# A graph layer on one Trainium2 core: edges of one destination packed three to a lane in place of two

## The chip, the cores and the metric

The kernel runs on one core of one Trainium2 chip. The metric is the time of one execution on the device in microseconds (us). TensorE is called PE below, VectorE DVE, ScalarE ACT, GpSimd POOL and SyncE SP. An engine name with a q behind it (SPq) is that engine's own instruction queue.

## The reference

There are 1250 nodes with rows of 1024 floats, 20000 edges `src -> dst`, and a type from 0 to 7 for each edge. Two layers follow each other, each with a residual and a layer norm.

```python
# layer 0: relational graph layer with a gate
out = x @ root + bias
for r in range(8):
    mask = (edge_type == r)
    sums = segment_sum(x[src] * mask[:, None], dst, num_segments=n)
    cnt = segment_sum(mask, dst, num_segments=n)
    out = out + (sums / maximum(cnt, 1.0)[:, None]) @ weight[r]
u = out
z = concatenate([u, x], axis=1) @ w_gate + b_gate
h = tanh(u) * z + x * (1.0 - z)
x = layernorm(x + h)
# layer 1: GCN, with a self loop at every node
dinv = rsqrt(deg)
msg = (x @ W)[src] * (dinv[src] * dinv[dst])[:, None]
x = layernorm(x + relu(segment_sum(msg, dst, num_segments=n) + b))
```

## The kernel before

**Products.** The kernel first forms `y = x @ weight[r]` for all eight types, a half of 512 columns at a time, and writes it to memory as rows. Then an edge's message is one row of `y`, picked by its type and source, times the share 1/cnt that belongs to its destination and type. Every product in 32-bit floats is done as three matmuls of a high and a low part (`xhi`, `xlo`, `whi`, `wlo`). A tile of 128 nodes by 512 columns is therefore 24 matmuls on PE (L790), and PE's program is written as a list of **steps**, each of them a half tile of 12 such matmuls (`half_tile`). Everything else that PE does is placed at the end of a step by tables from step to work (`spread`). DVE and ACT walk the same steps in programs of their own and come `LEAD` = 2 steps earlier with messages. ACT copies a finished tile out of PSUM (`evac`, L1095) and makes `whi` of the next weights (L1088), DVE makes `wlo` (L1310).

**Sorting the edges.** Early on, DVE and PE sort the edges by destination. All edges of one destination are put on lanes (partitions) of a group of 128 destinations. Two edges of one destination share a lane: 128 lanes by two edges are a **pair**. `NPAIR` = 92 pairs hold all edges whatever the draw, `ETILES` = 2 * 92 = 184 is the number of records per lane, and unused places hold an index out of range (`FAR`), for which a gather moves nothing.

**Counting (steps 150 to 215).** For layer 1 a matrix of counts, source by destination, is summed up. POOL makes a one-hot tile of the sources (`src_hot`, L685), DVE one of the destinations (`count_hot`, L1525), PE multiplies the two (`count_pair`, L802: four matmuls of 320 columns a pair), ACT takes the result as integers (`take_counts`, L1132), and DVE adds them to `COUNT` (`count_add`, L1535).

**Messages (run 0 at steps 229 to 314 for the left half of the columns, run 1 at steps 324 to 412 for the right half).** For each pair POOL issues two indirect DMAs (L711) that gather 128 rows of `y` each into one of eight row buffers `raw`. ACT scales the first row by its edge's share (`scale_row`, L1113). DVE multiplies the second by its share and adds the first (`msg_sum`, L1542). Then it makes the one-hot tile of the destinations, `ONEHOT` (L1544). ACT makes the high part of the sum (`msg_high`, L1119), DVE the low part (`msg_low`, L1549). PE multiplies both by the one-hot tile (`message_pair`, L813 and L814: one matmul of 512 columns each), and DVE adds PE's result to the sums `U` three pairs later (`msg_add`, L1556).

**What orders it.** Row buffer r is gathered into again once row r has been used: the first row of a pair when `msg_sum` has read it (`pair_summed`), the second when `msg_low` has (`msg_split`). So POOL is at most eight rows ahead. ACT's `message` scales the first row of the *next* pair before it makes the high part of this one. Ahead of the first pair of run 0, DVE waits for a small transposition (`deg_max_turned`, L925) that PE does at the start of step 229. Run 1 reads rows that exist only when the last tile of the right half, that of step 319, is stored; and its gathers start no earlier than that store. Behind the messages come the gate product (L886), the gate (L952), the product of layer 1 (L979) and its sums (L1045).

Of the kernel before, what the change touches and what calls it, by code (L numbers as in the profile page):

```python
# [28 lines left out]
I16 = mybir.dt.int16  # L29
# [4 lines left out]
P = 128  # L34
# [8 lines left out]
NPAIR = (E // 2 + N // 2 + NT * (P - 1)) // P  # L43
ETILES = 2 * NPAIR
# [10 lines left out]
HIGH_CELL = 1 << 16  # L55
SPLIT = 1024
EXACT = 256
AHEAD = 2
HOTS = 8
EARLY = 5  # L60
SLOTS = 4

# [14 lines left out]
RUN1_FROM, RUN1_TO = 324, 413  # L77
# [6 lines left out]

def spread(start, end, count=NPAIR):
# [6 lines left out]
COUNT_GROUPS = NPAIR // 2  # L92
COUNT_PAIRS = {s: range(2 * these.start, 2 * these.stop) for s, these in spread(COUNT_FROM, COUNT_TO, COUNT_GROUPS).items()}
RUN0_PAIRS = spread(RUN0_FROM, RUN0_TO)
RUN1_PAIRS = spread(RUN1_FROM, RUN1_TO)


def ahead(pairs):

    return {s - LEAD: these for s, these in pairs.items()}  # L100
# [14 lines left out]
def gnn_resnorm_kernel(nc, x, src, dst, edge_type, w_rel, w_root, b_root, w_gate, b_gate, w_gcn, b_gcn, out):  # L115
# [8 lines left out]
    count_d = dram("edge_count", (P, NT * NPAD), I16)  # L124
# [6 lines left out]
    with ctx:  # L131
# [56 lines left out]
        CIN = [place("CIN0", [P, NPAD], I16, "raw_w"), place("CIN1", [P, NPAD], I16, "stage")]  # L188

        U = WORK[:, 0:NT * HW].rearrange("p (g n) -> p g n", g=NT)  # L190
        COUNT = WORK[:, 0:NT * NPAD // 2].bitcast(I16).rearrange("p (g n) -> p g n", g=NT)
# [76 lines left out]
        O_HALF = field("O_HALF", [EPART, CHUNK], I32)  # L268
# [9 lines left out]
        GROUP = small("GROUP", [1, NPAIR], I32)  # L278
        DINV = small("DINV", [P, NT], F32)

        SRC_LOC = place("SRC_LOC", [P, ETILES], F32, "early")
        CELL = place("CELL", [P, ETILES], F32, "early", 4 * ETILES)
        ADDR = place("ADDR", [EPART, ECOL], I32, "early", 8 * ETILES)
        COLS = place("COLS", [P, NCOL], F16, "early", 8 * ETILES + 4 * ECOL)
# [11 lines left out]
        PAIRSUM = place("PAIRSUM", [1, 2, NPAIR], F32, "onehot", 1024)  # L296
# [51 lines left out]
        got = [sem(f"got{b}") for b in range(2 * SLOTS)]  # L348
        row_scaled = sem("row_scaled")
        pair_summed = sem("pair_summed")  # L350
        msg_hi = sem("msg_hi")
        msg_split = sem("msg_split")
        pair_ready = sem("pair_ready")
        pair_done = sem("pair_done")
        pair_added = sem("pair_added")
# [108 lines left out]
        def _(sp):  # L464
# [56 lines left out]
            def load_gate(t):  # L521
                if t == 0:
                    sp.wait_ge(pair_done, 2 * NPAIR)
# [38 lines left out]
            sp.wait_ge(msg_split, 2 * NPAIR - 2)  # L562
            load_root(0)
            sp.wait_ge(msg_split, 2 * NPAIR - 1)
# [727 lines left out]
        def _(dve):  # L1292
# [274 lines left out]
            def count_step(pair):  # L1567
                group, odd = divmod(pair, 2)
                if odd:
                    return  # L1570
# [330 lines left out]
```

## Time and profile before

| | before |
|---|---|
| median of 3 runs | 1624.74 us (1624.61 to 1626.62) |
| the profiled execution | span 1624.1 us from the first to the last instruction; granted PE clock 0.996 of full speed |
| PE busy | 98% of the span |
| DVE, ACT, POOL busy | 69%, 35%, 52% |
| chain that ended last | 93% on PE |

The profile gives the span of its execution; what lies outside it is taken as the 0.6 us between that span and the median. A PE that is shown as busy is not yet a PE that is needed at every instant, because a matmul's time as shown overlaps with that of the next one. Where its matmuls follow each other without an idle gap, the distance between their starts is what one costs.

### The profile page before, as it was taken

What the parts mean: (1) busy time and instruction counts of PE and PEld (TensorE: products, weight loads), DVE (VectorE), ACT (ScalarE), POOL (GpSimd) and SP (SyncE); (2) the same over time, 40 slices, a digit from 0 to 9 for tenths busy, and PEclk for the clock granted to TensorE, in tenths of its full rate; (3) what the DMA queues carried; (4) which work ended last, traced back from release to release, by engine and by line L of the source; (5) the groups of instructions that cost most, each with busy time, mean ns of one, the idle gap of its engine ahead of it and who ended that gap; (6) DMA issues with size and microseconds to landing.
All of it is one profiled execution on the core that took longest, in us unless ns stands there. A gap on an engine that the chain in (4) does not pass through costs nothing.

```text
span 1624.1 us, 23696 instructions
## 1 busy us (share of the span) xinstructions
PE 1597.2 (98%) x7947; PEld 1308.5 (81%) x7947; DVE 1127.3 (69%) x1894; ACT 575.9 (35%) x963; POOL 838.1 (52%) x823
## 2 busy tenths in 40 slices
PE   8999999999999999999999999999999998999997
PEld 7888888888877777788888888888888876888886
DVE  4856655655457667748878785778788869767486
ACT  4211111111133434425655553555555652222000
POOL 1000777777766666537777772777676601222000
PEclk9999999999999999999999999999999999999999
DMA  6322444444322121267777874777778785666643
GB/s 236 103 87 81 129 115 131 112 108 141 83 79 79 59 78 64 67 229 226 247 234 219 250 222 143 236 238 228 231 227 279 273 292 171 238 215 225 267 145 117
DMA packets 122124, 280.34 MB, mean 173 GB/s; under 512 B 23143, under 2 KB 24407, under 8 KB 121873
## 3 DMA queue, kind: packets, MB, share of 16 engines
q0 software_dynamic: 38256, 104.17, 22.3%
q1 hardware_dynamic: 46912, 98.19, 18.8%
q10 hardware_dynamic: 36832, 76.44, 12.5%
q8 instruction: 65, 1.06, 0.3%
q14 instruction: 59, 0.48, 0.1%
HBM read 209.97 MB, written 83.10 MB: 180 GB/s over the span
## 4 chain that ended last, share of the span: by engine, by line
PE 93%; DVE 3%; DMA 2%; issue 1%; ACT 0%; POOL 0%; SPq 0%; ACTq 0%; DVEq 0%; POOLq 0%
PE PG L790 67%; PE PG L979 6%; PE PG L1045 5%; PE PM L802 3%; PE PG L886 3%; PE PM L813 3%; PE PM L814 3%; PE PG L952 2%; DMA y<-STAGE 1%; PE PM L848 1%; PE PM L831 1%; PE PM L772 0%; DMA WRAW<-in_L_gnn_weight_dram 0%; PE PM L961 0%; DMA XROWS<-in_x_dram 0%
## 5 line engine op out<-in xcount | busy, mean ns | idle before, releaser
L790 PE MATMUL PG<-WHI,XHI 128*128 128x512 f32 x1600 | 631.7, 395 | 2.2 <-DVE WLO L1310 2.2
L790 PE MATMUL PG<-WHI,XLO 128*128 128x512 f32 x1600 | 623.5, 390 | 0.0
L790 PE MATMUL PG<-WLO,XHI 128*128 128x512 f32 x1600 | 623.0, 389 | 0.0
L790 PEld LDWEIGHTS PG<-WHI,XHI 128*128 128x128 f32 x1600 | 300.9, 188 | 64.5 <-issue 2.5
L790 PEld LDWEIGHTS PG<-WHI,XLO 128*128 128x128 f32 x1600 | 300.6, 188 | 63.7
L790 PEld LDWEIGHTS PG<-WLO,XHI 128*128 128x128 f32 x1600 | 301.0, 188 | 60.0
L1095 ACT ACTIVATE STAGE<-PG 128x512 f32<-128x512 f32 x200 | 119.1, 596 | 452.8 <-PE PG L790 452.6
L1310 DVE TENSOR_TENSOR WLO<-WRAW,WHI 128x512 fp32r<-128x512 f32 x176 | 122.1, 694 | 223.4 <-ACT WHI L1088 223.1
L711 POOL DMA_INDIRECT WORK<-y,REC x184 | 202.7, 1102 | 91.7 <-issue 49.3
L658 POOL DMA_INDIRECT records<-RREC,IDX x160 | 210.1, 1313 | 61.0 <-issue 43.7
L711 POOL DMA_INDIRECT RAW<-y,REC x184 | 204.2, 1110 | 70.4 <-issue 48.0
L685 POOL TENSOR_SCALAR SRCHOT<-IOTA,SRC_LOC 128x128 bf16<-128x128 f16 x184 | 148.6, 822 | 79.7 <-PE PM L802 79.6
L1556 DVE TENSOR_TENSOR WORK<-WORK,PM 128x512 f32 x184 | 125.3, 681 | 11.5 <-PE PM L814 9.6
L746 POOL TENSOR_TENSOR RSTD<-VAR,MINUS_HALF 128x1 f32<-128x1 f32 x20 | 11.0, 550 | 212.5 <-DVE VAR L1701 212.5
L1535 DVE TENSOR_TENSOR WORK<-WORK,TALLY 128x1280 int16 x92 | 76.7, 833 | 60.5 <-DVE WORK L1535 35.0
L1088 ACT ACTIVATE WHI<-WRAW 128x512 fp32r<-128x512 f32 x176 | 110.1, 626 | 7.7 <-DMA WRAW<-in_L_gnn_weight_dram 3.6
L1132 ACT ACTIVATE TALLY<-PM 128x640 int32<-128x640 f32 x92 | 59.9, 703 | 121.1 <-PE PM L802 121.1
L1119 ACT ACTIVATE SPHI<-WORK 128x512 fp32r<-128x512 f32 x92 | 57.9, 629 | 66.9 <-DVE WORK L1542 66.7
L644 POOL DMA_DIRECT2D EDGE_ROWS<-edge_rows x10 | 7.7, 769 | 141.8 <-DVE ADDR L1459 94.7
L1119 ACT ACTIVATE SPHI<-RAW 128x512 fp32r<-128x512 f32 x92 | 57.9, 630 | 63.9 <-DVE RAW L1542 63.0
L1549 DVE TENSOR_TENSOR SPLO<-WORK,SPHI 128x512 fp32r<-128x512 f32 x92 | 64.3, 699 | 20.0 <-ACT SPHI L1119 17.4
L1113 ACT ACTIVATE RAW<-RAW,REC 128x512 f32<-128x512 f32 x92 | 66.0, 717 | 33.6 <-DMA RAW<-y,REC 29.5
(265 smaller groups left out, 2257.3 us busy)
## 6 DMA issues: line engine op xcount, KB each, us to landing
y<-STAGE ACTq DMA_DIRECT2D x220, 256.0 KB
WRAW<-in_L_gnn_weight_dram SPq DMA_DIRECT2D x128, 256.0 KB, 3.2
EDGE_ROWS<-edge_rows POOLq DMA_DIRECT2D x10, 1000.0 KB, 6.2
WRAW<-in_L_gnn_w_gate_dram SPq DMA_DIRECT2D x32, 256.0 KB, 4.2
WORK<-y SPq DMA_DIRECT2D x15, 512.0 KB, 4.4
WORK<-x SPq DMA_DIRECT2D x10, 512.0 KB, 4.7
WORK<-in_x_dram SPq DMA_DIRECT2D x9, 512.0 KB, 3.7
XROWS<-in_x_dram SPq DMA_DIRECT2D x9, 512.0 KB
```

What stands on the lines that cost most here:

```text
L658: pool.indirect_dma_start(out=rec_d, out_offset=bass.IndirectOffsetOnAxis(ap=IDX[0:EPART, b, j:j + 1], axis=0), in_=RREC[0:EPART, b, j, :] ...
L685: last = nc.gpsimd.tensor_scalar(SRCHOT[:, tile % HOTS, :], IOTA[:, 0:P], SRC_LOC[:, tile:tile + 1], None, ALU.is_equal)
L711: pool.indirect_dma_start(out=raw[tile % (2 * SLOTS)], out_offset=None, in_=y_d[0:(run + 1) * YROWS, :], in_offset=bass.IndirectOffsetOnAx ...
L790: last = pe.matmul(PG[:, bank, :], lhs[:, k, t * P:(t + 1) * P], rhs[:, j % 2, k, :], start=(k == 0 and n == 0), stop=(k == KT - 1 and n = ...
L979: last = pe.matmul(PG[:, h_bank(t) + h, :], lhs[:, k * P:(k + 1) * P], rhs[:, k, h * HW:(h + 1) * HW], start=(m == 0 and n == 0), stop=(m ...
L1045: last = pe.matmul(PG[:, 2 * b + h, :], c_hi[:, s * P:(s + 1) * P], part[:, h * HW:(h + 1) * HW], start=(s == order[0] and n == 0), stop=( ...
L1088: nc.scalar.activation(high[:, k, :], raw[:, k, :], ACT.Copy).then_inc(w_hi, 1)
L1095: nc.scalar.activation(STAGE[:, b, :], PG[:, jt % 4, :], ACT.Copy).then_inc(evac_done, 1)
L1119: nc.scalar.activation(sp_hi[:, slot, :], raw[2 * slot + 1], ACT.Copy).then_inc(msg_hi, 1)
L1310: V.tensor_tensor(low[:, k, :], raw[:, k, :], high[:, k, :].bitcast(F32), ALU.subtract).then_inc(w_split, 1)
L1535: V.tensor_tensor(acc, acc, TALLY[:, n % 2, :].bitcast(I16), ALU.add).then_inc(cells_added, 1)
L1556: V.tensor_tensor(acc, acc, PM[:, n % SLOTS, :], ALU.add).then_inc(pair_added, 1)
```

## The change

Three edges of one destination now share a lane. The groups of three are called tris. `NTRI` = 68 of them hold all edges, so there are 3 * 68 = 204 rows to gather per run. Per tri DVE adds two rows to the first (`add_row`, once for each), there is one `ONEHOT`, one high and one low part, one pair of message matmuls and one `msg_add`. A count step is six matmuls of 320 columns. The one-hot buffers of the counting are 6 in place of 8, and counting goes tri by tri where it went by two pairs. The eight row buffers are now a ring over all rows of both runs, and two rows of a tri come free by `row_added`, the third by `msg_split`. The steps of the count and of run 0 are as before; run 1 begins at step 325 in place of 324. The counts are kept as unsigned 16-bit numbers in doubled form for half of the destinations, which `DINV_OUT` takes back.

```diff
+PER = 3
+NTRI = ((E + (PER - 1) * N) // PER + NT * (P - 1)) // P
+ETILES = PER * NTRI
-HOTS = 8
+HOTS = 2 * PER
+RAWS = 8
-RUN1_FROM, RUN1_TO = 324, 413
+RUN1_FROM, RUN1_TO = 325, 413
...
-            def src_hot(pair):
-                after(pool, cells_done, pair + AHEAD + 1 - HOTS // 2)
-                for e in range(2):
+            def src_hot(tri):
+                after(pool, cells_done, tri - 1)
+                for e in range(PER):
...
+            def row_free(row):
+                tri, e = divmod(row, PER)
+                if e == PER - 1:
+                    after(pool, msg_split, tri + 1)
+                else:
+                    after(pool, row_added, (PER - 1) * tri + e + 1)
...
                 for tile in range(ETILES):
-                    pair = tile // 2 + run * NPAIR
-                    after(pool, msg_split if tile % 2 else pair_summed, pair - (SLOTS - 1))
+                    row_free(run * ETILES + tile - RAWS)
                     pool.sem_inc(passed_pool, 1)
+                    slot = (run * ETILES + tile) % RAWS
                     pool.indirect_dma_start(
...
-            def message_pair(pair, slot, run):
+            def message_tri(tri, run):
+                slot, tri = tri % SLOTS, tri + run * NTRI
+                pe.wait_ge(tri_ready, tri + 1)
+                pe.wait_ge(msg_split, tri + 1)
+                after(pe, tri_added, tri + 1 - SLOTS)
                 pe.matmul(PM[:, slot, :], ONEHOT[:, slot, :], sp_hi[:, slot, :], start=True, stop=False)
...
+            def msg_high(tri, run):
+                n, row = run * NTRI + tri, run * ETILES + PER * tri + PER - 1
+                act.wait_ge(row_added, (PER - 1) * (n + 1))
...
+            def message(tri, run):
+                if tri == 0:
+                    scale_row(0, run)
+                if tri + 1 < NTRI:
+                    scale_row(tri + 1, run)
+                msg_high(tri, run)
...
+            def add_row(tri, e, run):
+                row, n = run * ETILES + PER * tri + e, run * NTRI + tri
+                this = raw[row % RAWS]
+                dve.wait_ge(got[row % RAWS], 16 * (row // RAWS + 1))
+                if e == 1:
+                    dve.wait_ge(row_scaled, n + 1)
+                else:
+                    dve.wait_ge(row_added, (PER - 1) * n + e - 1)
+                V.scalar_tensor_tensor(this, this, REC[:, PER * tri + e, 1:2].bitcast(F32), raw[(row - 1) % RAWS], ALU.mult,
+                                       ALU.add).then_inc(row_added, 1)
...
+            def message_step(tri, run):
+                if run == 1 and tri == 0:
+                    start_sums(1)
+                add_row(tri, 1, run)
+                msg_hot(tri)
+                for e in range(2, PER):
+                    add_row(tri, e, run)
+                if tri >= SLOTS - 1:
+                    msg_add(tri - (SLOTS - 1), run)
+                msg_low(tri, run)
```

On DVE, in run 0, two pairs in a row stood like this before (`WORK` and `RAW` hold the row buffers, `SPHI` and `SPLO` the high and low parts, `PM` PE's result):

```order
L1542 SCALAR_TENSOR_TENSOR WORK<-WORK,REC 128x512 [waits row_scaled,got1]
L1544 TENSOR_SCALAR ONEHOT<-IOTA,REC 128x128
L1529 TENSOR_LOAD GROUP
L1529 ISA x2
L1556 ISA [waits pair_done]
L1556 TENSOR_TENSOR WORK<-WORK,PM 128x512
L1549 TENSOR_TENSOR SPLO<-WORK,SPHI 128x512 [waits msg_hi,pair_added]
L1542 SCALAR_TENSOR_TENSOR WORK<-WORK,REC 128x512 [waits row_scaled,got3]
L1544 TENSOR_SCALAR ONEHOT<-IOTA,REC 128x128
```

At the same place DVE now has, for one tri and the start of the next:

```order
L1575 SCALAR_TENSOR_TENSOR WORK<-WORK,REC 128x512 [waits row_scaled,got2]
L1579 TENSOR_SCALAR ONEHOT<-IOTA,REC 128x128
L1575 SCALAR_TENSOR_TENSOR WORK<-WORK,REC 128x512 [waits row_added,got3]
L1549 TENSOR_LOAD GROUP
L1549 ISA x2
L1592 ISA [waits tri_done]
L1592 TENSOR_TENSOR WORK<-WORK,PM 128x512
L1585 TENSOR_TENSOR SPLO<-WORK,SPHI 128x512 [waits msg_hi,tri_added]
L1575 SCALAR_TENSOR_TENSOR RAW_69<-RAW_69,REC 128x512 [waits row_scaled,got5]
```

A second addition with a wait for its own row stands between `ONEHOT` and `msg_add`, and one `ONEHOT` now covers three gathered rows.

On POOL, behind the first eight gathers of run 0, the gathers waited like this before:

```order
L711 DMA WORK<-y,REC 128x512 [waits pair_summed]
L711 DMA WORK<-y,REC 128x512 [waits msg_split]
L711 DMA WORK<-y,REC 128x512 [waits pair_summed]
L711 DMA WORK<-y,REC 128x512 [waits msg_split]
L711 DMA RAW_69<-y,REC 128x512 [waits pair_summed]
```

They now stand like this:

```order
L724 DMA WORK<-y,REC 128x512 [waits row_added] x2
L724 DMA WORK<-y,REC 128x512 [waits msg_split]
L724 DMA WORK<-y,REC 128x512 [waits row_added]
L724 DMA RAW_69<-y,REC 128x512 [waits row_added]
L724 DMA RAW_69<-y,REC 128x512 [waits msg_split]
```

Every third gather waits for a low part, where every second one did; there are 204 of them a run, where there were 184.

## Rows read from the trace of the kernel before

**Rows 1.** The page: engines' busy time and the chain that ended last
```profile
PE 1597.2 (98%) x7947; PEld 1308.5 (81%) x7947; DVE 1127.3 (69%) x1894; ACT 575.9 (35%) x963; POOL 838.1 (52%) x823
PE 93%; DVE 3%; DMA 2%; issue 1%; ACT 0%; POOL 0%; SPq 0%; ACTq 0%; DVEq 0%; POOLq 0%
```

**Rows 2.** Windows: window, its us, busy us (xcount) by engine, PEclk, DMA
```profile
725.00:999.00 274.00, 273.85 (x1209) 226.62 (x1208) 222.41 (x401) 157.26 (x261) 198.26 (x176) 1.00 0.71 219
1023.00:1311.00 288.00, 288.00 (x1287) 238.31 (x1286) 234.27 (x419) 167.55 (x280) 194.52 (x179) 1.00 0.78 243
```

**Rows 3.** Chain in order of time, start, us: counting, run 0, between runs
```profile
465.00 1.10 PE PM L802 x8
...
729.12 0.23 PE PM L814
729.34 2.72 PE PG L790 x12
732.06 0.23 PE PM L813
...
998.17 0.23 PE PM L813
998.39 0.23 PE PM L814
998.62 27.20 PE PG L790 x120
```

**Rows 4.** Timeline of POOL, run 0: start, us, instruction, idle before
```profile
702.98 1.11 POOL L711 DMA_INDIRECT WORK<-y,REC  x1 [2.43 <-issue]
...
708.32 0.99 POOL L711 DMA_INDIRECT RAW<-y,REC  x1 [0.30 <-issue]
709.62 1.00 POOL L711 DMA_INDIRECT RAW<-y,REC  x1 [0.30 <-issue]
...
724.74 1.41 POOL L711 DMA_INDIRECT WORK<-y,REC  x1 [11.52 <-DVE WORK L1542]
...
733.88 1.24 POOL L711 DMA_INDIRECT RAW<-y,REC  x1 [0.30 <-DVE SPLO L1549]
...
983.12 1.48 POOL L711 DMA_INDIRECT RAW<-y,REC  x1 [0.30 <-issue]
```

**Rows 5.** Windows, POOL's L711 alone: window, us, busy us (xcount)
```profile
724.00:854.00 130.00, 101.82 (x89) 1.00 0.76 232
854.00:983.00 129.00, 95.22 (x87) 1.00 0.72 221
1015.00:1145.00 130.00, 98.42 (x90) 1.00 0.77 235
1145.00:1296.00 151.00, 101.45 (x95) 1.00 0.80 255
```

**Rows 6.** Windows, DVE's L1544 (ONEHOT) alone, same first window
```profile
724.00:854.00 130.00, 13.30 (x45) 1.00 0.76 232
```

**Rows 7.** Timeline of DVE, start of run 0
```profile
703.62 4.95 DVE L1634 COPY WORK<-WORK 128x4608 f32<-128x4608 f32 x1 [1.65 <-DMA WORK<-in_L_gnn_bias_dram]
...
732.89 0.69 DVE L1549 TENSOR_TENSOR SPLO<-RAW,SPHI 128x512 fp32r<-128x512 f32 x1
733.50 0.74 DVE L1542 SCALAR_TENSOR_TENSOR WORK<-WORK,REC 128x512 f32<-128x512 f32 x1
734.16 0.28 DVE L1544 TENSOR_SCALAR ONEHOT<-IOTA,REC 128x128 fp32r<-128x128 f16 x1
734.36 0.68 DVE L1556 TENSOR_TENSOR WORK<-WORK,PM 128x512 f32 x1
```

**Rows 8.** Chain in order of time: the first message of run 0
```profile
723.14 0.76 DVE WORK L1542
...
723.93 0.64 ACT SPHI L1119
...
724.59 0.70 DVE SPLO L1549
...
725.43 0.47 PE PM L813
```

**Rows 9.** The view of DMA issues: the gathers, median us to landing
```profile
WORK<-y,REC POOLq DMA_INDIRECT x184, 4.5
```

**Rows 10.** Timeline of POOL between the runs
```profile
1000.76 1.03 POOL L718 DMA_DIRECT2D agg<-WORK  x1 [16.16 <-DVE WORK L1556]
1015.74 1.06 POOL L711 DMA_INDIRECT WORK<-y,REC  x1 [4.33 <-DMA y<-STAGE]
```

**Rows 11.** Timeline of PE: the last two message pairs of run 1
```profile
1309.80 0.39 PE L813 MATMUL PM<-SPHI,ONEHOT 128*128 128x512 f32 x1
1310.25 0.39 PE L813 MATMUL PM<-SPHI,ONEHOT 128*128 128x512 f32 x1
```

**Rows 12.** The page: groups, busy us, mean ns of one, idle before
```profile
L685 POOL TENSOR_SCALAR SRCHOT<-IOTA,SRC_LOC 128x128 bf16<-128x128 f16 x184 | 148.6, 822 | 79.7 <-PE PM L802 79.6
...
L1535 DVE TENSOR_TENSOR WORK<-WORK,TALLY 128x1280 int16 x92 | 76.7, 833 | 60.5 <-DVE WORK L1535 35.0
...
L1113 ACT ACTIVATE RAW<-RAW,REC 128x512 f32<-128x512 f32 x92 | 66.0, 717 | 33.6 <-DMA RAW<-y,REC 29.5
```

**Rows 13.** DVE's L1525, duration ns min/median/max
```profile
L1525 DVE TENSOR_SCALAR DSTHOT<-COLS,CELL,WORTH x184: 433/443/497, 454.4 to 683.2; 128x640 bf16<-128x640 f16 x184
```

More of the change, by code:

```diff
@@ L28 @@
 I32 = mybir.dt.int32
-I16 = mybir.dt.int16
+U16 = mybir.dt.uint16
 ALU = mybir.AluOpType
@@ L82, with spread @@
 STEPS_ALL = STEPS_GEMM + 2 * NT
-def spread(start, end, count=NPAIR):
+def spread(start, end, count=NTRI):
     steps = end - start
@@ L89, in spread, with ahead @@
     return {start + k: range(bounds[k], bounds[k + 1]) for k in range(steps)}
[L92 to L100, printed above, removed]
+COUNT_TRIS = spread(COUNT_FROM, COUNT_TO)
+RUN0_TRIS = spread(RUN0_FROM, RUN0_TO)
+RUN1_TRIS = spread(RUN1_FROM, RUN1_TO)
+def ahead(tris):
+    return {s - LEAD: these for s, these in tris.items()}
 class Chain:
@@ L899, in half_tile, with steps @@
                 gate_upper(t, h)
-            def steps(start, end, pairs={}, pair_step=None):
+            def steps(start, end, tris={}, tri_step=None):
                 for s in range(start, end):
                     half_tile(s)
-                    for pair in pairs.get(s, ()):
-                        pair_step(pair, pair)
-            pe.sem_inc(cells_done, AHEAD)
+                    for tri in tris.get(s, ()):
+                        tri_step(tri)
             turn_x(0)
@@ L1157, in tile_end, with steps @@
                     store_y(i, jt)
-            def steps(start, end, pairs={}, run=None):
+            def steps(start, end, tris={}, run=None):
                 for s in range(start, end):
@@ L1165, in steps @@
                         store_upper(s - STEPS_GEMM - 1)
[L1166 removed]
+                    for tri in tris.get(s, ()):
                         if run is None:
[L1168 removed]
+                            take_counts(tri)
                         else:
[L1170 to L1172 removed]
+                            message(tri, run)
             x_high(0)
@@ L1547, in msg_low, with count_hot @@
-            def msg_low(pair, slot, run):
-                dve.wait_ge(msg_hi, run * NPAIR + pair + 1)
-                V.tensor_tensor(sp_lo[:, slot, :], raw[2 * slot + 1], sp_hi[:, slot, :].bitcast(F32),
+            def count_hot(tri):
+                after(dve, cells_done, tri - 1)
+                for e in range(PER):
+                    tile = PER * tri + e
+                    last = V.tensor_scalar(DSTHOT[:, tile % HOTS, :], COLS[:, :], CELL[:, tile:tile + 1], WORTH[:, tile:tile + 1],
+                                           ALU.is_equal, ALU.mult)
+                last.then_inc(hot_ready, 1)
@@ L1607, in upper_gate_work, with steps @@
                     u0_low(t)
-            def steps(start, end, pairs={}, pair_step=None, messages={}, run=None):
+            def steps(start, end, tris={}, tri_step=None, messages={}, run=None):
                 for s in range(start, end):
-                    for pair in pairs.get(s, ()):
-                        pair_step(pair)
+                    for tri in tris.get(s, ()):
+                        tri_step(tri)
                     if s % 2 == 0 and s % SUBSTEPS > 0:
```

263 lines of the change are left out of this document (118 added, 145 removed).

## The prediction, made before the changed kernel ran

> **What bounds the kernel now.** I read the page's chain first. It lies on PE for 93% of the span, and PE is busy for 98% [rows 1]. A busy PE could still be a PE that is spread out by waits, so I looked at the windows of the two message runs: 273.85 of 274.00 us in run 0 and 288.00 of 288.00 us in run 1, at full clock [rows 2]. There is no idle time to win there; only fewer matmuls make these stages shorter. What one costs is read from the chain in order of time. A half tile of 12 is 2.72 us, so a 512-column matmul is 0.227 us, and each of the two of a message pair is 0.23 us. A count step of 8 is 1.10 us, so a 320-column matmul is 0.1375 us [rows 3].
>
> Then comes the engine that the change loads more, POOL. It is busy for 52% of the whole [rows 1], which hides two things. First, a gather takes 1.00 us and then 0.30 us of issue, 1.30 us in all, when DVE does little beside it [rows 4]. Second, gathers take longer beside the message work: 101.82 us for 89 of them in the first 130 us of run 0, which is 1.144 us each and 1.44 us with the 0.30. With the other three windows it is 396.9 us for 361, 1.10 us each [rows 5]. A run has 184 gathers. At 1.40 to 1.44 us that is 258 to 265 us of POOL in a run of 274 us. So POOL is nearly full in these stages already.
>
> **What the change removes on PE.** There are 92 - 68 = 24 fewer groups per run, 2 matmuls each: 48 * 0.227 = 10.9 us per run, 21.8 us in both. The number of half tiles stays.
>
> **What it adds on PE.** Counting has 68 * 6 = 408 matmuls in place of 92 * 4 = 368, 40 more at 0.1375 us = 5.5 us. They come in some 66 packets in place of 46, and a packet has a small cost of its own that these rows don't separate. I take 6 us, between 5.5 and 7. If nothing else happened, the kernel would come to 1624.7 - 21.8 + 6 = 1609 us.
>
> **What it adds on POOL.** 204 gathers per run in place of 184. This decides the sum, so I worked out the pitch p of the new gathers, from start to start. Its floor is 1.30 us [rows 4]. The excess over 1.00 us has a pattern. The gather at 733.88 takes 1.24 us, and DVE's `ONEHOT` (0.28 us) begins 0.28 us into it [rows 4, 7]; the gather at 708.32 takes 0.99 us though DVE's copy of 4.95 us runs at its start. I charge the excess to `ONEHOT`. In the first window the excess is 101.82 - 89 = 12.8 us for 45 of them, 0.285 us each [rows 5, 6]. Over all four windows it is 396.9 - 361 = 35.9 us for about 180 (one for two gathers), 0.20 us each. The new kernel has one `ONEHOT` for three gathers, so p is 1.30 + 0.285 / 3 = 1.395 or 1.30 + 0.20 / 3 = 1.366. I take 1.395, because in the first window POOL is never held up, which is the state in which it will have to work throughout. If all DVE work slowed a gather alike, p would stay at 1.44.
>
> The Trainium skill, "SBUF — State Buffer", section "Who interferes with whom", says that a `tensor_scalar` in a two-port mode locks POOL out of writing descriptors until it ends, and that a `tensor_tensor` does not hold them up. By that rule the added DVE additions cost POOL nothing and p comes down with the number of `ONEHOT`s, to the 1.395 above; without it the sum would be made with 1.44 and come out some 18 us higher. The gather with `ONEHOT` inside it agrees with the rule; no row here isolates an addition.
>
> **Run 0.** The first eight gathers go out early. Then POOL waits 11.52 us, because the first row comes free only with DVE's first addition [rows 4], which waits for PE's transposition at step 229. Nothing of that changes, so on the old clock (the 6 us of counting left aside) gather number 8 again starts at 724.74, and the last, number 203, at 724.74 + 195 p. From its start to PE's matmul it takes 4.5 us to land [rows 9] and 2.3 us for addition, high part and low part, from 723.14 to 725.43 [rows 8]: 6.8 us. With p = 1.395 PE gets the last tri at 724.7 + 272.0 + 6.8 = 1003.6. Before, PE did the last pair at 998.17 [rows 3]. PE alone could be there at 998.2 - 24 * 0.454 = 987.3. So the removed matmuls are replaced by a PE that waits, from early in the run on, and the stage ends 5.4 us later than before.
>
> **Run 1.** The gathers start when the last right-half tile is stored, at 1015.74 [rows 10]. This is tied to PE's step 319 and not to run 0's gathers: run 0's sums are stored from 1000.76 on and are out before. The last tri reaches PE at 1015.7 + 203 * 1.395 + 6.8 = 1305.7. Before, the last pair was at 1310.25 [rows 11]; PE alone could be there at 1310.3 - 10.9 = 1299.4. Run 1 ends 4.5 us earlier. It fares better than run 0 because its gathers start at once and go on: in run 0 POOL loses 11.52 us behind the eighth. That run 1 starts one step later doesn't enter, since POOL sets its end.
>
> **What I cost at nothing.** DVE in a run: 24 groups fewer save 24 * (0.74 + 0.28 + 0.68 + 0.69) = 57 us, 68 second additions cost 50 us, so its 222 of 274 us falls to 215 [rows 2, 7]. Its cover is the time in which it waits for rows; if that went, each added addition would cost up to its 0.74 us, 50 us a run. The row buffers: the third row of a tri comes free after the next gather (1.4), its landing (4.5), the scaling of that row (0.72, [rows 12]), high and low part (1.4), 8.0 us together; it is gathered into again 8 * 1.395 = 11.2 us on. This leaves 3 us for a late landing. In the counting, POOL has 3 * 0.82 = 2.5 us of one-hots per tri and DVE 3 * 0.44 + 0.83 = 2.2 us [rows 12, 13], against 2.72 + 0.83 = 3.5 us on PE, with two tris of buffers. Two steps hold two tris, where PE may wait for about 0.5 us. If the unsigned addition took twice its 0.83 us, DVE would have 3.0 us, still less than 3.5.
>
> **The sum.** 6 + 5.4 - 4.5 = +6.9 us on the span of 1624.1, and so 1631.6 us on the median of 1624.74, with which this execution agrees to 0.6 us. I say 1632. Each 0.01 us in p moves it by 195 + 203 = 398 gathers, 4.0 us. The sum is zero at p = 1.378.
>
> **Rivals.**
> (A) The forecast, POOL sets the end of both runs with p from 1.375 to 1.42: 1624 to 1642 us. For it speaks the first window; chance 0.52.
> (B) The other sign: `ONEHOT` hits fewer gathers once POOL has no other work to wait for. It is the mean of all four windows, p = 1.366. Then run 0 ends at 997.9 (-0.3) and run 1 at 1299.8 (-10.5), and the sum is 6 - 10.8 = -4.8, 1620 us. The more p falls towards 1.30, the more it comes to 1609 us, PE alone. It decides from p below 1.378. Against it: three of its four windows contain gathers that had time. Chance 0.24.
> (C) The pitch does not fall or rises, because the additions slow gathers too or rows come free late: p from 1.42 to 1.50, 1642 to 1673 us; at 1.44 it is 724.7 + 280.8 + 6.8 = 1012.3 (+14.1) and 1314.8 (+4.6), so 1649 us. For it: the ring has only 3 us to spare. Chance 0.16.
> (D) PE waits in the counting too, with six one-hot buffers for eight: at 0.1 to 0.3 us for each of 68 tris, 7 to 20 us more than the forecast, 1639 to 1652 us. Against it: POOL was idle for 79.7 us there [rows 12]. Chance 0.08.
>
> **How the numbers follow.** A measurement of this kernel tells about 0.2% (3.2 us) from no change. Slower by more needs p over about 1.386: two thirds of A, C and D, 0.60. Within 0.2%: the rest of A and the upper edge of B, 0.17. Faster: 0.23. The range of 8 in 10 leaves out p below 1.33 and above 1.44: 1613 to 1650 us. A alone is 1624 to 1642.
>
> **What would show it.** In the changed profile: PE idle before the message matmuls, put down to DVE's low part, some 16 us in run 0 and 6 us in run 1, where it was nothing; POOL's gathers without a wait over 0.3 us from the ninth on, 1.09 us long on average; ACT and DVE waiting for gathers to land; run 0's end 5 us later and run 1's end 4.5 us earlier, on PE's own steps; the counting about 6 us longer. Wrong it would be if POOL showed waits for `row_added` or `msg_split` (C), if PE had no idle time in run 1 (B), or if PE waited between steps 150 and 216 (D).

## The result, and the profile after

The changed kernel takes 1658.95 us (median of 4 runs, 1657.05 to 1660.25) against 1624.81 us for the kernel before on the same chip (1624.61 to 1626.62): a ratio of 1.0205, 95% interval 1.0193 to 1.0217. The profiled execution has a span of 1658.1 us against 1624.1, at a granted clock of 0.994. The direction was the one forecast; the size, 34 us where I had said 7, lies outside the range.

From the page: engines' busy time, and the chain by engine.
```profile
PE 1601.9 (97%) x7891; PEld 1289.0 (78%) x7891; DVE 1119.6 (68%) x1868; ACT 497.2 (30%) x843; POOL 887.5 (54%) x883
PE 67%; DMA 11%; DVE 8%; issue 7%; ACT 3%; POOL 3%; POOLq 0%; DVEq 0%; SPq 0%; ACTq 0%
```
The chain answers to the second line of [rows 1]: PE has fallen from 93% to 67% of it, and DMA, DVE and issue have come in, 26% together. PE's busy time has even risen by 5 us, which says nothing by itself. The windows do. Here are step 229 to step 315 (run 0) and step 320 to the last message (run 1): window, its us, busy us of PE, PEld, DVE, ACT and POOL, PEclk, DMA.
```profile
729.83:1017.87 288.04, 273.23 (x1171) 216.60 (x1170) 221.87 (x375) 123.98 (x212) 219.66 (x196) 1.00 0.68 206
1031.51:1339.29 307.78, 295.68 (x1283) 236.64 (x1282) 236.54 (x391) 135.09 (x232) 227.80 (x205) 0.99 0.75 232
```
PE filled every microsecond of both stages [rows 2]. Now it is idle for 14.8 us in the first and 12.1 us in the second. The groups of PE's line 827 (the first matmul of a message, line 813 before) in these two windows show where: after the bar stands the idle time before them.
```profile
L827 PE MATMUL PM<-SPHI,ONEHOT 128*128 128x512 f32 x68 | 28.9, 425 | 14.4 <-issue 14.2
L827 PE MATMUL PM<-SPHI,ONEHOT 128*128 128x512 f32 x68 | 28.4, 417 | 11.9 <-issue 11.3
```
So PE waits for messages. What feeds them is POOL's line 724, the gather (711 before). First its timeline (start, us, idle before), then windows from the ninth gather of run 0 on and over run 1, for this line alone:
```profile
732.75 1.00 POOL L724 DMA_INDIRECT WORK<-y,REC  x1 [12.24 <-DVE WORK L1575]
...
1011.80 1.00 POOL L724 DMA_INDIRECT WORK<-y,REC  x1 [0.30 <-issue]
1022.13 1.03 POOL L731 DMA_DIRECT2D agg<-WORK  x1 [9.34 <-DVE WORK L1592]
...
1036.48 1.06 POOL L724 DMA_INDIRECT RAW<-y,REC  x1 [4.36 <-DMA y<-STAGE]
```
```profile
732.00:1012.00 280.00, 218.87 (x196) 1.00 0.69 210
1036.00:1330.00 294.00, 226.86 (x204) 0.99 0.76 236
```
The 195 pitches (from the start of one gather to the start of the next) from 732.75 to 1011.80 are 1.431 us each; those of run 1, 203 from 1036.48 to 1329.35, are 1.443. Each window ends inside its last gather; with the 0.80 and 0.35 us that lie beyond, a gather takes 219.67 / 196 = 1.121 us and 227.21 / 204 = 1.114 us. POOL works through both runs almost without a wait: behind the ninth gather of run 0 one idle time, and in run 1 four, exceed the 0.30 us of issue by more than 0.05. One of the four is long, 4.23 us ahead of the ninth gather of run 1; it comes back below. Otherwise this is the state that I forecast for POOL. The gathers themselves are longer than I had taken.

Where the 34.0 us went, each stage measured on PE's own steps in both traces:

```
stage                               before    after   change   forecast
start to step 150                   455.55   454.85    -0.7       0
step 150 to 229 (counting)          266.74   274.98    +8.2      +6
step 229 to 315 (run 0)             276.17   288.04   +11.9      +5.4
step 315 to 320                      13.60    13.64     0.0       0
step 320 to last message (run 1)    298.2    307.8     +9.6      -4.5
last message to end                 313.9    318.8     +4.9       0
```

Some twenty of the 27 us that I missed lie in the two runs.

### The profile page after: what moved, and what is told of

Same layout as the page of the kernel before. It is cut to its first block, busy times and chain, and to the rows that moved or that the text cites. A ratio compares the mean times of both kernels' runs of the same rounds, so it can differ in the third digit from the quotient of the medians.

```text
span 1658.1 us, 23202 instructions
## 1 busy us (share of the span) xinstructions
PE 1601.9 (97%) x7891; PEld 1289.0 (78%) x7891; DVE 1119.6 (68%) x1868; ACT 497.2 (30%) x843; POOL 887.5 (54%) x883
## 4 chain that ended last, share of the span: by engine, by line
PE 67%; DMA 11%; DVE 8%; issue 7%; ACT 3%; POOL 3%; POOLq 0%; DVEq 0%; SPq 0%; ACTq 0%
PE PG L803 46%; PE PG L992 6%; DMA RAW<-y,REC 5%; PE PG L1058 5%; DMA WORK<-y,REC 4%; PE PM L816 3%; PE PG L965 2%; DVE RAW L1575 2%; DVE WORK L1575 2%; DMA y<-STAGE 2%; POOL records L663 1%; ACT SPHI L1134 1%; PE PG L900 1%; ACT WHI L1101 1%; PE PM L827 1%
## 5 line engine op out<-in xcount | busy, mean ns | idle before, releaser
L724 POOL DMA_INDIRECT RAW<-y,REC x204 | 229.5, 1125 | 71.0 <-issue 46.3
L724 POOL DMA_INDIRECT WORK<-y,REC x204 | 225.5, 1105 | 77.2 <-issue 45.7
L690 POOL TENSOR_SCALAR SRCHOT<-IOTA,SRC_LOC 128x128 bf16<-128x128 f16 x204 | 154.0, 771 | 83.2 <-PE PM L816 83.2
L1555 DVE TENSOR_TENSOR WORK<-WORK,TALLY 128x1280 uint16 x68 | 56.6, 833 | 86.7 <-ACT TALLY L1147 85.9
L1592 DVE TENSOR_TENSOR WORK<-WORK,PM 128x512 f32 x136 | 93.5, 688 | 12.1 <-issue 6.7
L1147 ACT ACTIVATE TALLY<-PM 128x640 int32<-128x640 f32 x68 | 48.1, 707 | 162.0 <-PE PM L816 161.8
L1127 ACT ACTIVATE WORK<-WORK,REC 128x512 f32<-128x512 f32 x68 | 49.1, 724 | 147.4 <-DMA WORK<-y,REC 146.6
L1127 ACT ACTIVATE RAW<-RAW,REC 128x512 f32<-128x512 f32 x68 | 49.2, 724 | 136.9 <-DMA RAW<-y,REC 135.3
L827 PE MATMUL PM<-SPHI,ONEHOT 128*128 128x512 f32 x136 | 57.3, 421 | 26.4 <-issue 25.5
L1544 DVE TENSOR_SCALAR DSTHOT<-COLS,CELL,WORTH 128x640 bf16<-128x640 f16 x204 | 79.3, 445 | 2.5
```

The lines of the kernel that those rows point to most:

```text
L690: last = nc.gpsimd.tensor_scalar(SRCHOT[:, tile % HOTS, :], IOTA[:, 0:P], SRC_LOC[:, tile:tile + 1], None, ALU.is_equal)
L724: pool.indirect_dma_start(out=raw[slot], out_offset=None, in_=y_d[0:(run + 1) * YROWS, :], in_offset=bass.IndirectOffsetOnAxis(ap=REC[:, t ...
L1127: nc.scalar.activation(raw[row % RAWS], raw[row % RAWS], ACT.Copy, scale=REC[:, PER * tri, 1:2].bitcast(F32)).then_inc(row_scaled, 1)
L1544: last = V.tensor_scalar(DSTHOT[:, tile % HOTS, :], COLS[:, :], CELL[:, tile:tile + 1], WORTH[:, tile:tile + 1], ALU.is_equal, ALU.mult)
L1592: V.tensor_tensor(acc, acc, PM[:, tri % SLOTS, :], ALU.add).then_inc(tri_added, 1)
```

## The second reading of the gathers

The row on which the prediction charged `ONEHOT` reads otherwise with one row more. In [rows 4, 7] the gather at 733.88 takes 1.24 us. `ONEHOT` begins inside it, but DVE's addition (line 1542) began at 733.50, before the gather, and ended at 734.24. If the gather stood still until then, all but 0.12 us of its 1.00 us would be left at 734.24, and it would take just the 1.24 us. I had looked only at what begins inside the gather. In the changed kernel's timeline (DVE and POOL, start and us) the same thing is plainer:
```profile
737.99 0.75 DVE L1575 SCALAR_TENSOR_TENSOR RAW<-RAW,REC 128x512 f32<-128x512 f32 x1
738.24 1.37 POOL L724 DMA_INDIRECT RAW<-y,REC  x1 [0.30 <-issue]
738.65 0.28 DVE L1579 TENSOR_SCALAR ONEHOT<-IOTA,REC 128x128 fp32r<-128x128 f16 x1
...
742.52 1.01 POOL L724 DMA_INDIRECT RAW<-y,REC  x1 [0.30 <-issue]
742.57 0.28 DVE L1579 TENSOR_SCALAR ONEHOT<-IOTA,REC 128x128 fp32r<-128x128 f16 x1
```
At 738.24 an addition is under way until 738.74 and the gather takes 0.37 us more than 1.00; at 742.52 only `ONEHOT` stands beside it and it takes 1.01.

**Theory 2** is therefore: an operation of DVE that reads two operands from SBUF (an addition of rows, the low part of a message or of the weights) and is under way when a gather starts holds the gather until it ends. Laid over all gathers of a trace, the rule is sharp. Caught gathers are those with such an operation that began more than 0.05 us before the gather and ended more than 0.124 us behind its start; the excess is what a gather takes over 1.000 us, and the rule's own figure is the operation's end less the gather's start less 0.124 us.

```
kernel                    gathers  caught  excess of the  excess of    charged to additions,
                                           caught, us     the rest     low parts, weights
before                      368     150      39.2          -0.4        14.6, 13.7, 10.9
after                       408     198      46.5           0.5        29.5, 13.9,  2.3
additions read PSUM (e2)    408      74      20.3           1.5           0, 14.4,  4.7
sum in PSUM (e4)            408       5       1.3          -0.9           0,    0,  1.3
```

In the changed kernel all but seven of the caught gathers agree with the rule to 0.01 us, and the gathers that it does not catch have 0.5 us of excess together. The seven have none either: there an addition had begun only 0.057 to 0.096 us before them. The 272 additions in place of 184 doubled their part, 14.6 to 29.5 us. (What is not listed is other two-operand sums of DVE, under 1.3 us.) But this is a pattern in traces in which all DVE work moves together; the runs have to take it apart.

**Theory 1** stays the prediction's: `ONEHOT` is what lengthens a gather. **Theory 3**: any DVE work does.

## The experiments

**Without ONEHOT.** The changed kernel, with this in `msg_hot`; the sums of all groups but the first four of a run go to wrong lanes.
```diff
+                if tri >= SLOTS:
+                    dve.sem_inc(tri_ready, 1)
+                    return
```


> The changed kernel, but VectorE builds ONEHOT only for the first four groups of each run (the later groups' sums are then taken by wrong lanes; all else is the same). Numbers are the pitch of POOL's gathers from the ninth of run 0 on, 1.431 us in the changed kernel, and the time, 1659 us there. Theory 1, that of the prediction: ONEHOT's building lengthens one gather in three by 0.285 us; the pitch falls to about 1.335 and the time to about 1620. Theory 2: a VectorE operation that reads two operands from SBUF (an added row, the low part, the weights' low part) holds a gather up until it ends, and ONEHOT only stands next to one; the pitch stays between 1.42 and 1.44 and the time between 1652 and 1660. Theory 3, any work of VectorE lengthens a gather in proportion to its time: ONEHOT is about a tenth of VectorE's work, the pitch falls by about 0.013 and the time by about 5.

Measured: 1657.25 us (ratio to before 1.0196, 1.0179 to 1.0213). The gathers' windows:
```profile
732.00:1006.00 274.00, 214.00 (x196) 1.00 0.70 214
1031.00:1324.00 293.00, 224.13 (x204) 1.00 0.76 237
```
With the rest of the last gathers, behind the windows' ends, that is 1.097 and 1.101 us a gather; the pitch is 1.402 and 1.439. Theory 1 wanted 1.335 and some 1620 us; it falls. The mean pitch fell by 0.016, about what theory 3 says too, so this run doesn't part theories 2 and 3. In run 0 the 1.402 lies below theory 2's 1.42 as well. Its rule catches 173 gathers in this trace, with 39.3 us of excess, and leaves 0.4 us to the others, so fewer caught gathers account for the lower pitch; why they are fewer is not shown.

**The additions read PSUM.** The changed kernel; the sums leave out a group's earlier rows.
```diff
-                V.scalar_tensor_tensor(this, this, REC[:, PER * tri + e, 1:2].bitcast(F32), raw[(row - 1) % RAWS], ALU.mult,
+                V.scalar_tensor_tensor(this, this, REC[:, PER * tri + e, 1:2].bitcast(F32), PM[:, tri % SLOTS, :], ALU.mult,
```


> The changed kernel, but both additions of a group take their second operand from the group's bank of PSUM in place of the row before in SBUF (so the sum leaves the earlier rows out; as many operations of VectorE, in the same places, with the same waits but for the contents). Theory 1 (ONEHOT) and theory 3 (any VectorE work): pitch 1.42 to 1.44, time 1655 to 1660. Theory 2 (two operands in SBUF): two of the three such operations of a group are gone; left is the low part, 0.745 us long, which at a random phase costs 0.745 squared over two pitches = 0.19 us a group, and the weights' low part; pitch 1.37 to 1.40, time about 1638 (0.05 of pitch by 4.0 us for each 0.01), between 1630 and 1646.

Measured: 1635.05 us (median of 6 runs, 1632.33 to 1640.39; 1.0054, 1.0036 to 1.0072), 24 us less than the changed kernel. In the profiled execution, the slowest of the six, the pitch is 1.368 and 1.391. The same place in the program as above, and the gathers' windows:
```profile
738.97 0.74 DVE L1575 SCALAR_TENSOR_TENSOR RAW<-RAW,REC,PM 128x512 f32<-128x512 f32 x1
739.23 1.00 POOL L724 DMA_INDIRECT RAW<-y,REC  x1 [0.30 <-issue]
```
```profile
733.00:1001.00 268.00, 206.60 (x196) 1.00 0.71 219
1025.00:1309.00 284.00, 214.24 (x204) 1.00 0.77 244
```
Again the gather starts 0.26 us into an addition, which lasts as long as before (0.74 us); it takes 1.00 us in place of 1.37. Nothing differs but where the second operand lies. And it is no single case: 102 gathers of this trace start over 0.1 us into such an addition with 0.2 us or more of it to come, and none of them takes more than 1.011 us. Theory 3 falls with theory 1, and theory 2 gave the time: 1638 forecast. (The low part lasts 0.69 us, not the 0.745 of the expectation.)

**The sum in PSUM.** This carries the finding to all operations of the message work and computes all that the reference does. The core of its diff (`row_free` follows it):
```diff
-                nc.scalar.activation(raw[row % RAWS], raw[row % RAWS], ACT.Copy,
+                after(act, tri_added, run * NTRI + tri + 1 - SLOTS)
+                nc.scalar.activation(PM[:, tri % SLOTS, :], raw[row % RAWS], ACT.Copy,
...
-                V.scalar_tensor_tensor(this, this, REC[:, PER * tri + e, 1:2].bitcast(F32), raw[(row - 1) % RAWS], ALU.mult,
+                V.scalar_tensor_tensor(acc, raw[row % RAWS], REC[:, PER * tri + e, 1:2].bitcast(F32), acc, ALU.mult,
...
-                V.tensor_tensor(sp_lo[:, slot, :], raw[row % RAWS], sp_hi[:, slot, :].bitcast(F32),
+                V.tensor_tensor(sp_lo[:, slot, :], PM[:, slot, :], sp_hi[:, slot, :].bitcast(F32),
```


> Computes all that the reference does. ScalarE writes the scaled first row of a group into the group's bank of PSUM, the two additions add there, and the high and the low part are read from there, so that no operation of the message stages but the weights' low part reads two operands from SBUF; rows come free at the scaling or the addition that reads them. Theory 2: pitch 1.31 to 1.34; run 0 then ends near 998 (the changed kernel's 1017) and run 1 takes some 286 us from step 320 (307.8): time 1612 to 1625. Theories 1 and 3: pitch 1.42 to 1.44, time 1652 to 1660.

Measured: 1745.47 us (1.0741, 1.0721 to 1.0761), some 125 us over what I expected. The gathers' windows, then two rows of the waits:
```profile
731.00:1044.00 313.00, 195.03 (x196) 0.99 0.62 187
1077.00:1410.00 333.00, 204.26 (x204) 0.99 0.67 207
```
```profile
ACT PM L1128 <- DVE WORK L1593: 397.1, 128, 3.7
...
DVE SPLO L1586 <- ACT SPHI L1135: 185.2, 134, 1.8
```
On the gathers' own time theory 2 was right: 195.03 us for 196, 1.00 each. But the pitch is 1.60 and 1.64, since POOL now waits. The first row above is the new wait that my edit made and that I had not priced: ScalarE's scaling writes the bank, so it waits until DVE has taken the bank's old sums (line 1593), 397.1 us in 128 waits. One turn in the timeline:
```profile
864.51 0.75 DVE L1576 SCALAR_TENSOR_TENSOR PM<-RAW,REC,PM 128x512 f32<-128x512 f32 x1
865.26 1.00 POOL L724 DMA_INDIRECT RAW<-y,REC  x1 [0.73 <-issue]
865.27 0.69 DVE L1593 TENSOR_TENSOR WORK<-WORK,PM 128x512 f32 x1
866.05 0.69 ACT L1128 ACTIVATE PM<-RAW,REC 128x512 f32<-128x512 f32 x1 [3.10 <-DVE WORK L1593]
...
866.68 0.58 ACT L1135 ACTIVATE SPHI<-PM 128x512 fp32r<-128x512 f32 x1
...
867.37 0.69 DVE L1586 TENSOR_TENSOR SPLO<-PM,SPHI 128x512 fp32r<-128x512 f32 x1 [1.41 <-ACT SPHI L1135]
```
Second addition, taking of the sums, scaling of the next group, high part, low part: five operations on two engines, one behind the other, and the next group's first addition comes only behind them. DVE stands idle for 1.41 us in each turn, and a turn lasts three pitches, 4.8 us, where three gathers need 3.9.

**The same with the largest degree turned at step 221** (PE's `deg_max_turned`, so that the ninth gather isn't held up).

> As the one with the sum in PSUM, and PE turns the largest degree at step 221 in place of 229, so that VectorE doesn't wait for it ahead of the first group and the ninth gather isn't held up 12 us behind the eighth. Computes all that the reference does. If theory 2 holds, run 0 is then bound by PE: 86 steps at 2.72 us and 68 groups at 0.454 = 265 us from step 229, which ends some 3 us before the one without this edit: 1610 to 1622, and 0 to 4 us under it. If the gathers still bound run 0, the 12 us come off its end, or as much of them as PE leaves.

Measured: 1741.66 us (1.0731, 1.0694 to 1.0769). No difference beyond the spread: the circle sets the pace. Twice more, below, this edit did nothing.

**The sums taken first.** In `message_step`, `msg_add(tri - (SLOTS - 1), run)` moves ahead of `add_row(tri, 1, run)`.

> Computes all that the reference does. The sum in PSUM once more; there every gather took 1.000 us, but ScalarE's scaling of the next group's first row waited for VectorE to take the sums out of that bank (198 us in each half of the rows), and VectorE took them only behind the two additions of the group before: a circle of scaling, two additions and the taking. Here VectorE takes the sums of the group three back ahead of its two additions, so that the scaling runs beside them. If that circle was the cause of the 1745 us, the gathers come to a pitch of 1.30 to 1.34 and run 0 and run 1 to PE's bound: 265 to 270 us from step 229 (changed kernel 288) and about 285 us from step 320 (307.8); time 1610 to 1622. If the bank's turn round (scaling, additions, split, PE, taking, four banks) is the limit by itself, the pitch stays over 1.40 and the time over 1650.

> Computes all that the reference does. As the one before, and PE turns the largest degree at step 221 in place of 229. If the gathers bound run 0, its end comes earlier by up to the 12 us for which the ninth gather waits; if PE does, by 3 us or less. 1606 to 1620.

Measured: 1671.13 us (1.027, 1.0251 to 1.0288), and 1671.44 us with the early turning. 74 us came back, so the circle was real; but run 0 still takes 290.2 us and run 1 315.4. My expectation missed what the move uncovers: nothing stands between the second addition and the low part any more, and DVE waits 0.67 us a group for the high part. Its own sequence, 4.3 us a group, is now the bound.

**The high part first.** The sums are taken behind the additions again, and the order of ScalarE is changed in their place; in the first and the third of these kernels DVE also builds `ONEHOT` of group n + 1 behind the low part of group n.
```diff
+                msg_high(tri, run)
                 if tri + 1 < NTRI:
                     scale_row(tri + 1, run)
-                msg_high(tri, run)
```


> Computes all that the reference does: the sum in PSUM as in the first such kernel (sums taken behind the two additions), but ScalarE writes a group's high part ahead of scaling the next group's first row, and VectorE builds ONEHOT of the next group behind the low part. Reason: in the kernel with the sums taken first, gathers were 1.005 us and VectorE's own sequence was the limit (two additions 1.51, the sums 0.69, the low part 0.69, ONEHOT 0.28, about 0.6 of weights' low parts a group at 0.69, and 0.67 waiting for the high part = 4.3 us a group, 68 groups = 290 us). Here the taking of the sums covers the wait for the high part, and the low part and ONEHOT cover the scaling: 3.6 us a group, under the 3.9 of three gathers and of PE. Expect gathers of 1.00 to 1.02 us, pitch 1.31 to 1.35, run 0 266 to 272 us, run 1 288 to 292, time 1610 to 1625. If the banks' turn round is the limit whatever the order, 1650 or more.

> Computes all that the reference does. The same without the move of ONEHOT: only ScalarE's order differs from the first kernel with the sum in PSUM (1745 us). If that order (the scaling, which waits for the sums to be taken, ahead of the high part) made the circle, nearly all of the 120 us go: VectorE waits some 0.2 us a group more than with the move of ONEHOT, 68 by 2 by 0.2 = 27 us at most where VectorE binds: 1612 to 1650.

> Computes all that the reference does. The first of these three with PE's turning of the largest degree at step 221. Nothing to 12 us less in run 0 where the gathers bind it; nothing where PE does: 1606 to 1625.

Measured: 1646.7 us (1.0132, 1.0108 to 1.0157), 1642.61 us for the swap alone (1.0098, 1.0077 to 1.0119) and 1644.68 us with the early turning (1.0102, 1.0061 to 1.0143). The swap took away some 100 us and `ONEHOT`'s place is worth nothing measurable. The swap alone lies within its range; the other two are 20 us and more over theirs, and one row of the first one's waits in run 1 points at a cause, which the next run tests:
```profile
DVE WLO L1325 <- ACT WHI L1101: 46.8, 37, 15.4
```
DVE takes the low part of the next unit's weights ahead of each step's group, and waits there for ScalarE's high part, which now stands behind the scaling: 46.8 us in run 1, with the next additions queued behind it.

**The weights' low part behind the group.** On top of the last, in DVE's `steps`:
```diff
+                    for tri in messages.get(s, ()):
+                        message_step(tri, run)
                     if s % 2 == 0 and s % SUBSTEPS > 0:
                         w_low_next(s // SUBSTEPS, s % SUBSTEPS // 2 - 1)
                     if s >= STEPS_GEMM - 12:
                         upper_gate_work(s)
-                    for tri in messages.get(s, ()):
-                        message_step(tri, run)
```


> Computes all that the reference does. The sum in PSUM with the high part ahead of the scaling and ONEHOT behind the low part (1647 us; gathers 1.01 to 1.02 us, pitch 1.349 and 1.402), and VectorE takes the weights' low part of a step behind that step's group in place of ahead of it. Reason: in that kernel VectorE waited 46.8 us in run 1 ahead of 37 of these low parts, 1.26 us each, for the weights' high part, which ScalarE makes behind the scaling and the evacuation, and the next group's additions stood behind that wait. Expect these waits under 10 us in run 1, pitch 1.31 to 1.35 in both runs, run 0 266 to 271 us, run 1 291 to 297, time 1615 to 1632. If VectorE's wait only moves to the high part of the group (ScalarE then makes it behind the evacuation), the time stays over 1635.

Measured: 1619.09 us (5 runs, 1618.42 to 1622.4) against 1626.19 before: 0.9958, 0.9944 to 0.9972. This computes all that the reference does and is faster than both kernels, than the one before by 7 us. First the two stages on PE's steps, then the gathers' windows, then DVE's group for the weights' low part in run 1:
```profile
731.12:998.62 267.50, 265.49 (x1171) 219.19 (x1169) 227.41 (x377) 127.46 (x213) 200.98 (x196) 1.00 0.72 223
1012.22:1303.93 291.71, 288.30 (x1284) 237.29 (x1282) 242.16 (x394) 138.86 (x234) 210.46 (x205) 1.00 0.78 248
```
```profile
731.00:992.00 261.00, 200.26 (x196) 1.00 0.73 226
1017.00:1289.00 272.00, 209.19 (x204) 1.00 0.80 254
```
```profile
L1325 DVE TENSOR_TENSOR WLO<-WRAW,WHI 128x512 fp32r<-128x512 f32 x37 | 25.4, 687 | 4.4 <-ACT WHI L1101 4.4
```
The wait fell from 46.8 to 4.4 us, the pitch is 1.336 and 1.337 with gathers of 1.025 and 1.029 us, and PE is idle for 2.0 and 3.4 us in the two stages. What excess is left comes mostly from the weights' low part, which still reads SBUF twice: 8.7 of the 11.0 us.

**That order alone.** The changed kernel, its sum in SBUF, with only the last diff.

> The changed kernel (sum in SBUF as it is there) with only VectorE's order of the last run: the weights' low part behind the step's group. Computes all that the reference does. If the gathers' delay by operations with two operands in SBUF is what binds the changed kernel, VectorE's waits cost nothing there and this does nothing: 1652 to 1662, gathers 1.10 to 1.12 us, pitch 1.42 to 1.44. If the order alone makes the gain of the last run, under 1635.

Measured: 1651.46 us (1.0156, 1.0139 to 1.0173), pitch 1.419 and 1.400. I had expected nothing, and it is 7 to 8 us. In run 1 none of POOL's idle times exceeds 0.35 us, so the 4.23 us ahead of the ninth gather are gone, and the caught gathers' excess is 41.8 us for 46.5. The other 32 us to the last kernel need the sum in PSUM, with ScalarE's order and `ONEHOT`'s place that go with it.

**Without the third gather.** The changed kernel, but POOL leaves out every third row's gather from the ninth of a run on, and the addition takes what lies in the buffer.
```diff
+                    if not gathered(run * ETILES + tile):
+                        continue
```


> The changed kernel without the gather of every third row from the ninth row of each run on (the third row of a group is then what lies in the buffer, so the sums are wrong; every operation of VectorE, ScalarE and PE stays). What it tells: the time when gathers bind nothing. The prediction's rows give for PE alone 86 half tiles at 2.72 us and 68 groups at 0.454 = 265 us from step 229 to 315, and 93 half tiles and 68 groups = 284 us from step 320 to the last message. All theories that put the loss on the gathers give 1612 to 1620; if VectorE's added work or PE's waits for it were the loss (a rival so far left out), the time stays over 1640.

Measured: 1610.37 us (0.9897, 0.9879 to 0.9915). The two stages on PE's steps:
```profile
730.35:995.20 264.85, 264.85 (x1171) 219.31 (x1170) 221.53 (x377) 127.97 (x212) 163.44 (x130) 1.00 0.59 179
1008.79:1298.50 289.71, 287.73 (x1283) 237.59 (x1282) 236.08 (x393) 139.72 (x234) 168.70 (x138) 1.00 0.66 205
```
With all of DVE's additions in place and a third of the gathers gone, PE is never idle in run 0, and the stage is the 265 us that its matmuls add up to. So the loss of the changed kernel hangs on the gathers' pace, not on DVE's time. Run 1 takes 289.7 us in place of the 284 expected: PE is idle for 2.0 us, and the expectation left out 32 small matmuls of 128 columns (packets of 4, 0.44 us each in the chain) that stand there before and after the change too. This run also gives about the most that these 68 groups could bring: 1610 us.

## Why the prediction was wrong in size

**PE's saving** was right. Where nothing else binds, run 0 is 264.9 us against 276.2, which is the 11 us of 48 matmuls.

**Counting** came to +8.2 us for +6. PE waited 0.3 us there, so rival D did not happen. The 40 matmuls are 5.5 us. The rest is in what a packet of counting matmuls costs beyond its own columns, read from the distances of PE's starts: a packet of eight and the half tile behind it are 1.12 us longer than a half tile alone, where its columns are 1.09; a packet of six is 0.88 us, where its columns are 0.82. That is 46 times 0.03 us before and 66 times 0.06 after. Why the smaller packet costs more is not shown.

**POOL as the bound** was right too, in both runs, and with it the direction of the change. So was its floor of 1.30 us: with the two-operand reads gone, gathers take 1.00 us.

**The step that failed** is "I charge the excess to `ONEHOT`", and with it the sentence that the added additions cost POOL nothing. Taking `ONEHOT` away left the time at 1657 us; taking the additions' second operand from PSUM brought it to 1635. The excess was 0.121 and 0.114 us a gather where I had 0.095. That is 195 * 0.026 = 5.0 us in run 0 and 203 * 0.019 = 3.8 us in run 1. The number looks like a small error, but its cause has the other sign: I had made the excess shrink with the number of `ONEHOT`s, while it grows with the number of additions. That 1.395 still came within 0.05 us of the measured pitch is luck; the prediction's other charge, 1.366, rested on the same reading and was further off. It is rival C's mechanism, "the additions slow gathers too", at C's pitch. Why `ONEHOT` looked guilty: it starts 0.66 us behind the start of each addition, so a gather that an addition holds up has `ONEHOT` inside it. An effect was charged to what begins within it and not to what was already running.

The Trainium skill, "SBUF — State Buffer", section "Who interferes with whom", has the rule that I needed a few lines from the one that I cited: "A DVE instruction with two SBUF inputs contends with a GpSimd instruction that reads SBUF", and a gather reads its list of rows, `REC`, from SBUF. The traces agree, with 1.37 against 1.00 us for the pair above. The sentence on `tensor_tensor` that I cited speaks of writing descriptors; for these gathers the measured 46.5 us of excess decide against drawing "costs nothing" from it.

**A second step failed**: that run 1's "gathers start at once and go on", and that its later start "doesn't enter". The pitch missed by more than the excess, by 0.036 us in run 0 (7.0 us in all) and 0.048 in run 1 (9.7 us). What the excess doesn't explain, 2.0 and 5.8 us, is idle time of POOL over the 0.30 us. Most of it in run 1 is the wait ahead of the ninth gather, 3.9 us over the 0.30. DVE and POOL of the changed kernel, then DVE before:
```profile
1043.73 0.69 DVE L1324 TENSOR_TENSOR WLO<-WRAW,WHI 128x512 fp32r<-128x512 f32 x1 [15.37 <-ACT WHI L1101]
1044.34 4.95 DVE L1653 COPY WORK<-WORK 128x4608 f32<-128x4608 f32 x1
1049.32 0.75 DVE L1575 SCALAR_TENSOR_TENSOR RAW<-RAW,REC 128x512 f32<-128x512 f32 x1
...
1050.92 1.00 POOL L724 DMA_INDIRECT RAW<-y,REC  x1 [4.23 <-DVE RAW L1575]
```
```profile
1014.25 4.95 DVE L1634 COPY WORK<-WORK 128x4608 f32<-128x4608 f32 x1 [5.34 <-DMA WORK<-in_L_gnn_bias_dram]
1021.54 0.75 DVE L1542 SCALAR_TENSOR_TENSOR WORK<-WORK,REC 128x512 f32<-128x512 f32 x1 [2.34 <-DMA WORK<-y,REC]
```
`spread` gives the first of run 1's 88 steps no tri, so the first one stands at step 326 and DVE comes to it at its step 324, where it came at 322 before. Step 324 has a low part of weights ahead of the messages. DVE waits 15.37 us for ScalarE to make the high part, then sets `U` to the bias (the copy of 4.95 us), and adds the first row only at 1049.32. Before, that copy was done before the first row had landed. In the run with DVE's order alone, the low part stands behind the group, and this wait is gone. So C's other half, rows that come free late, did happen, once.

**Run 1** was forecast 14.1 us too early. 9.7 us are the pitch, with the ninth gather's wait in it. The first gather came 4.97 us behind step 320 in place of 3.68, 1.3 us, again behind a store of `y` as in [rows 10]. From the last gather's start to PE took 9.9 us in place of 6.8, 3.1 us. In run 0 it took 5.5, so the 6.8 was fair as a mean only.

**The tail** is 4.9 us longer, which I had at nothing. The chain of the changed kernel there passes through stores that ScalarE makes one behind the other:
```profile
1340.65 6.75 DMA y<-STAGE
...
1348.11 7.13 DMA y<-STAGE
...
1355.95 5.79 DMA y<-STAGE
...
1362.46 6.14 DMA y<-STAGE
```
Before, two such waits stood in the chain, 6.26 and 7.62 us. The tail is 314.7 us in the kernel of 1619 us, 315.0 in the changed kernel with DVE's order alone, 310.4 without the third gathers, and 320.1 in the kernel with the sums taken first. I can't say what sets it: the tail's own program is the same in all of them, and no run isolates it.

## What to carry to other kernels

When an instruction's duration varies, line up what is already running on the other engines at its start, not only what begins inside it; then check the suspicion on the instances that have no excess, here the gathers of 1.00 us. An edit that adds a two-operand SBUF operation to VectorE beside a stream of gathers pays for it on POOL, and one operand in PSUM avoids that; but an accumulator in PSUM ties its bank to the engine that drains it, so write down the circle of waits and the order of each engine before pricing it. Saving PE time pays only down to the next engine's pace, here 3 gathers a group. And when a stage's first group moves by a step or two, look at what the engines then do ahead of it.

## What the runs showed of the hardware

An indirect gather on POOL that starts while VectorE reads two operands from SBUF ends 0.124 us earlier than 1.00 us after that operation's end; the same operation with one operand in PSUM leaves it at 1.00 us (1.37 against 1.00 us at the same offset of 0.26 us). How long before the gather the operation must have begun depends on it: low parts held a gather from about 0.05 us on; of the additions that began 0.05 to 0.10 us ahead of one in the changed kernel seven didn't and one did; those that began 0.12 us or more ahead did. One that begins after the gather's start doesn't hold it: 134 gathers of the changed kernel have such an operation begin inside them and none held before, and none takes more than 1.008 us. The operation itself lasts the same, 0.74 to 0.75 us, with its second operand in SBUF or in PSUM.
